# A graph network's node projection written out block by block, with gathers that wait for those of the last block, and half of the map-row gathers moved

## Time and profile before

| what | value |
|---|---|
| time, median of 3 runs | 4004.64 us (3991.43 to 4008.65) |
| the profiled execution | 4039.1 us, its span 4037.4 us |
| DVE busy | 2246.1 us, 56% of the span |
| POOL busy | 2168.0 us, 54% |
| PE busy | 2352.2 us, 58% |
| ACT busy | 1625.7 us, 40% |
| mean granted TensorE clock | 0.80 of 2.4 GHz |

### The profile page before, as it was taken

How to read it: one execution, slowest core, us unless ns; L and a number is a source line. 1 busy time by engine, 2 the same in 40 slices (tenths; PEclk the granted TensorE clock), 3 DMA queues, 4 the chain that set the end, 5 groups by cost and what they waited for, 6 DMA issues and landing times. The chain is left out here.

```text
span 4037.4 us, 57894 instructions
## 1 busy us (share of the span) xinstructions
PE 2352.2 (58%) x13633; PEld 1865.0 (46%) x13633; DVE 2246.1 (56%) x7631; ACT 1625.7 (40%) x3515; POOL 2168.0 (54%) x1921
## 2 busy tenths in 40 slices
PE   1136899899897664455646557775635433444333
PEld 1023676667677553354546445444624322333222
DVE  4145998899997665323422448885676323333223
ACT  0006999999995663222422323323421222222100
POOL 3628765566554770152055245555820488788755
PEclk9998999999999786587678668887866666666666
DMA  2140132233321543642455363333413433332243
GB/s 62 28 174 24 43 97 91 85 108 90 95 68 45 135 129 86 160 115 78 127 145 138 86 178 99 93 89 89 113 29 90 119 72 72 73 73 64 50 142 113
DMA packets 569016, 380.34 MB, mean 94 GB/s; under 512 B 51389, under 2 KB 511942, under 8 KB 568386
## 3 DMA queue, kind: packets, MB, share of 16 engines
q1 hardware_dynamic: 510050, 329.99, 27.7%
q0 software_dynamic: 56000, 46.29, 6.1%
q10 hardware_dynamic: 2720, 1.23, 0.2%
HBM read 249.08 MB, written 153.32 MB: 100 GB/s over the span
## 5 line engine op out<-in xcount | busy, mean ns | idle before, releaser
L1147 POOL DMA_INDIRECT p_ends_state<-t_d,p_ends_ix x300 | 315.6, 1052 | 543.9 <-issue 243.7
L806 POOL TENSOR_TENSOR a_rs<-a_ve,w_neg_half 128x16 f32<-128x16 f32 x113 | 330.4, 2924 | 244.8 <-DVE a_ve L742 214.9
L1367 PE MATMUL p_pm<-w_aug,p_ht 128*128 128x130 f32 (+1 forms) x1600 | 331.8, 329 | 173.0 <-ACT p_ht L1321 117.2
L832 ACT ACTIVATE a_nr<-a_xb,a_nm,a_rs 128x128 f32<-128x128 f32 x882 | 371.6, 490 | 26.1 <-POOL a_nm L808 26.1
L1367 PEld LDWEIGHTS p_pm<-w_aug,p_ht 128*128 128x128 f32 x1600 | 275.7, 234 | 194.9 <-issue 137.3
L1983 POOL DMA_INDIRECT e_a<-t_d,e_ix x200 | 211.7, 1059 | 269.7 <-DMA e_a<-t_s 206.9
L894 PE MATMUL a_ps<-w_ident,a_nr 128*128 128x128 f32 x1568 | 248.1, 282 | 127.8 <-ACT a_ht L840 46.9
L902 PE MATMUL a_ps<-a_ht,w_aug 128*128 128x512 f32 x588 | 315.6, 622 | 2.4 <-DVE a_ht L709 2.4
L894 PEld LDWEIGHTS a_ps<-w_ident,a_nr 128*128 128x128 f32 x1568 | 181.6, 144 | 276.7 <-issue 245.1
L709 DVE TENSOR_TENSOR a_ht<-a_ps,a_ht 128x512 f32<-128x512 f32 x294 | 203.1, 694 | 137.4 <-ACT a_ps L847 119.2
L1708 PE MATMUL c_pq<-layer_src,c_sel 128*128 (+1 forms) x800 | 194.3, 420 | 126.7 <-ACT c_sel L1679 83.5
(11 more groups left out here) (359 smaller groups left out, 6657.2 us busy)
## 6 DMA issues: line engine op xcount, KB each, us to landing
t_s<-p_ends_state SPq DMA_DIRECT2D x100, 256.0 KB
c_a<-t_d SPq DMA_DIRECT2D x100, 256.0 KB
t_d<-c_a SPq DMA_DIRECT2D x100, 256.0 KB
a_xa<-in_x SPq DMA_DIRECT2D x98, 256.0 KB
out<-a_xb SPq DMA_DIRECT2D x98, 256.0 KB, 2.0
p_ends_state<-t_s SPq DMA_DIRECT2D x75, 256.0 KB
p_ends_state<-t_d SPq DMA_DIRECT2D x75, 256.0 KB
t_acc<-q_zt SPq DMA_DIRECT2D x3, 2171.5 KB
```

The source lines that it names most:

```text
L806: nc.gpsimd.tensor_tensor(RS[:, z, :], VE[:, z, :], w["neg_half"][:, None, 0:J].to_broadcast([P, LNS, J]), ALU.pow).then_inc(s_rstd.sem, 1)
L832: last = nc.scalar.activation(NR[k][:, T.at(NORM[k], 2), cols(j)], normed_rows(T, k)[:, cols(j)], ACT.Identity, bias=NM[:, T.at(1, SHORT), ...
L1147: eng.indirect_dma_start(out=self.A[:, g, SRC, j, :], out_offset=None, in_=self.t[self.dst_table], in_offset=bass.IndirectOffsetOnAxis(ap= ...
L1367: last = nc.tensor.matmul(PM[side][:, j, 0:CW], HT[:, g, side, j * C:(j + 1) * C], rhs, start=side == SRC, stop=True)
```

## The change

- `project` is written out: all 25 blocks of each engine in straight code, no loop, no registers. The ring A has 7 blocks, the buffers behind it 3. SP issues all seven loads first; then, for each block b, store(b) and load(b + 6), and the xs rows of block b + 3.
- Overlay gathers read their index straight from `map_ix`; the copies L1139 are gone. Before the four gathers of block b POOL waits for the block's loads and, for each of the four columns j, for `s_over[j]` to reach 16 b: all four gathers of block b - 1 have landed.
- The inverse root moves from POOL to DVE: a new class `Moments` computes it with integer arithmetic on the float's bits as a first value and three Newton steps, in 12 steps (13 instructions) of 128 x 8 elements. Eight of the steps stand each behind one of the next block's eight statistics, four behind every second of its aggregates. A step waits for the one before it.
- ACT now normalises both sides (8 instructions a block, relu included for "first"); DVE writes both `layer_src` and `layer_dst` with the bias added (`hold`); the bias products on PE are gone. DVE's order is, for "first" and "normed": statistics with Newton steps, residual (lag 4), holds (lag 3); for "plain": residual (lag 1), holds (lag 0).
- The map-row gathers of `project` r = 0 are the first 50 alone, two per block, each pair behind the normalised destination side of a block. The other 50 stand on POOL in the `aggregate` phase of r = 0, two per block of that phase. They write straight into the int32 table `found`, so the casts are gone from `project`; `rows_found` runs after that aggregate phase and copies three more columns to float.

The diff, cut to its core:

```diff
@@ -477,11 +477,12 @@
                 ins_.then_inc(s_v, 1)
                 eng.wait_ge(s_v, n[0])
-            done(v.tensor_copy(k["map_ix"][:, :], f["found"][:, 0:T, 0]))
-            done(v.tensor_copy(OWNER[:, :], f["found"][:, 0:T, 1]))
+            done(v.tensor_copy(k["map_ix"][:, :], f["found"][:, :, 0]))
+            done(v.tensor_copy(OWNER[:, :], f["found"][:, :, 1]))
             for j in range(1, J):
-                done(v.tensor_tensor(OWNER[:, :], OWNER[:, :], f["found"][:, 0:T, 1 + j], ALU.min))
+                done(v.tensor_copy(TMP[:, :], f["found"][:, :, 1 + j]))
+                done(v.tensor_tensor(OWNER[:, :], OWNER[:, :], TMP[:, :], ALU.min))
             done(v.tensor_tensor(OWN[:, :], OWNER[:, :], f["number_f"][:, :], ALU.is_equal))
             done(v.tensor_scalar(TMP[:, :], k["src_col"][:, :], float(-SKIP), None, ALU.add))
...
+    def newton(self, eng, b, step):
+        v, g = self.nc.vector, b % self.ring
+        ve, half, square, y = self.var_eps[:, g, :], self.half[:, g, :], self.square[:, g, :], self.rstd[:, g, :]
+        if step == 0:
+            eng.wait_ge(self.s_moments, b + 1)
+            v.tensor_scalar(ve, self.moments[:, g, :, 1], LN_EPS, None, ALU.add).then_inc(self.s_newton, 1)
+            return
+        eng.wait_ge(self.s_newton, b * (self.STEPS - 1) + step)
+        if step == 1:
+            v.tensor_scalar(half, ve, -0.5, None, ALU.mult)
+            v.tensor_scalar(y.bitcast(I32), ve.bitcast(I32), -0.5, 1597463007.0, ALU.mult, ALU.add).then_inc(self.s_newton, 1)
+        elif step == self.STEPS - 1:
+            v.scalar_tensor_tensor(self.shift[:, g, :], self.moments[:, g, :, 0], -1.0, y, ALU.mult, ALU.mult).then_inc(self.s_shift, 1)
+        elif step % 3 == 2:
+            v.tensor_tensor(square, y, y, ALU.mult).then_inc(self.s_newton, 1)
+        elif step % 3 == 0:
+            v.tensor_tensor(square, square, half, ALU.mult).then_inc(self.s_newton, 1)
+        else:
+            v.scalar_tensor_tensor(y, square, 1.5, y, ALU.add, ALU.mult).then_inc(self.s_newton, 1)
+    def turn(self, eng, rows, b, last):
+        v = self.nc.vector
+        step = 0
+        for n in range(self.n):
+            if b <= last:
+                ins_ = v.bn_stats(self.stats[:, b % self.ring, n, :], rows(n))
+                if n == self.n - 1:
+                    ins_.then_inc(self.s_stats, 1)
+            if b and step < self.STEPS:
+                self.newton(eng, b - 1, step)
+                step += 1
+        if b <= last:
+            eng.wait_ge(self.s_stats, b + 1)
+        for n in range(self.n):
+            if b <= last:
+                ins_ = v.bn_aggr(self.moments[:, b % self.ring, n, :], self.stats[:, b % self.ring, n, :])
+                if n == self.n - 1:
+                    ins_.then_inc(self.s_moments, 1)
+            if n % 2 and b and step < self.STEPS:
+                self.newton(eng, b - 1, step)
+                step += 1
+        assert not b or step == self.STEPS
...
+            def load(b):
+                g = b % RING
+                if b >= RING:
+                    eng.wait_ge(s_out[g], (uses(b) - 1) * OUTS)
+                    eng.wait_ge(s_mm[DST], b - RING + 1)
+                for side in (SRC, DST):
+                    eng.dma_start(A[:, g, side, :, :], block_rows(t[tables[side]], b)).then_inc(s_load[g], 16)
+            def load_x(b):
+                if b >= SHORT:
+                    eng.wait_ge(s_plus, b - SHORT + 1)
+                eng.dma_start(XS[:, b % SHORT, :, :], block_rows(t["xs"], b)).then_inc(s_xs[b % SHORT], 16)
...
+            for b in range(RING):
+                load(b)
+                if plus_x and b < SHORT:
+                    load_x(b)
+            for b in range(BLOCKS):
+                store(b)
+                if b and b - 1 + RING < BLOCKS:
+                    load(b - 1 + RING)
+                if plus_x and b + SHORT < BLOCKS:
+                    load_x(b + SHORT)
+            for g in range(RING):
+                eng.wait_ge(s_out[g], OUTS * len(range(g, BLOCKS, RING)))
+        if overlay:
+            @block.gpsimd
+            def _(eng):
+                for b in range(BLOCKS):
+                    g = b % RING
+                    eng.wait_ge(s_load[g], uses(b) * 32)
+                    if b:
+                        for j in range(J):
+                            eng.wait_ge(s_over[j], 16 * b)
+                    for j in range(J):
+                        eng.indirect_dma_start(out=A[:, g, SRC, j, :], out_offset=None, in_=t[f"d{r}"],
+                                               in_offset=bass.IndirectOffsetOnAxis(ap=k["map_ix"][:, b * J + j:b * J + j + 1], axis=0),
+                                               bounds_check=EP - 1, oob_is_err=False).then_inc(s_over[j], 16)
+        if first:
+            @block.gpsimd
+            def _(eng):
+                for n in range(0, T // 2):
+                    eng.wait_ge(s_normed[DST], n // 2 + 1)
+                    eng.indirect_dma_start(out=f["found"][:, n, :], out_offset=None, in_=t["maps"].rearrange("(n a) o -> n (a o)", a=WORDS),
+                                           in_offset=bass.IndirectOffsetOnAxis(ap=f["map_at"][:, n:n + 1], axis=0),
+                                           bounds_check=NODES - 1, oob_is_err=False).then_inc(s_found, 16)
+                eng.wait_ge(s_found, 16 * (T // 2))
...
+            def hold(b):
+                for side in (SRC, DST):
+                    eng.wait_ge(s_mm[side], b + 1)
+                    v.tensor_tensor(held(("src", "dst")[side], b)[:, :, 0:CW], PM[side][:, :, 0:CW], wide, ALU.add).then_inc(s_keep[side], 1)
+            def residual(b):
+                g, grow = b % RING, UP[:, b % SHORT, :, :] if sigmoid else held("src", b)[:, :, 0:C]
+                if sigmoid:
+                    eng.wait_ge(s_sig, b + 1)
+                else:
+                    eng.wait_ge(s_keep[SRC], b + 1)
+                if plus_x:
+                    eng.wait_ge(s_xs[b % SHORT], (b // SHORT + 1) * 16)
+                    v.tensor_tensor(grow, grow, XS[:, b % SHORT, :, :], ALU.add).then_inc(s_plus, 1)
+                    eng.wait_ge(s_plus, b + 1)
+                there(eng, b, SRC)
+                v.tensor_tensor(A[:, g, SRC, :, :], A[:, g, SRC, :, :], grow, ALU.add).then_inc(s_next, 1)
+            holds, residuals = (3, 4) if norm else (0, 1)
+            for n in range(BLOCKS + residuals):
+                if norm and n <= BLOCKS:
+                    if n < BLOCKS:
+                        there(eng, n)
+                    mo.turn(eng, lambda m: A[:, n % RING, m // J, m % J, :], n, BLOCKS - 1)
+                if 0 <= n - residuals:
+                    residual(n - residuals)
+                if 0 <= n - holds < BLOCKS:
+                    hold(n - holds)
+            def apply(b):
+                g, m = b % RING, b % SHORT
+                eng.wait_ge(mo.s_shift, b + 1)
+                if normed and b >= SHORT:
+                    eng.wait_ge(s_mm[DST], b - SHORT + 1)
                 for side in (SRC, DST):
+                    for j in range(J):
+                        n = side * J + j
+                        rows = A[:, g, side, j, :]
+                        last = nc.scalar.activation(NR[:, m, side, j, :] if normed else rows, rows, ACT.Identity if normed else ACT.Relu,
+                                                    bias=mo.shift[:, m, n:n + 1], scale=mo.rstd[:, m, n:n + 1])
+                    last.then_inc(s_normed[side], 1)
...
@@ -1600,6 +1665,19 @@
+        if first:
+            s_found = sem("found")
+            @block.gpsimd
+            def _(eng):
+                for n in range(T // 2, T):
+                    if n >= T // 2 + 4:
+                        eng.wait_ge(s_next, (n - T // 2 - 2) // 2)
+                    eng.indirect_dma_start(out=f["found"][:, n, :], out_offset=None, in_=t["maps"].rearrange("(n a) o -> n (a o)", a=WORDS),
+                                           in_offset=bass.IndirectOffsetOnAxis(ap=f["map_at"][:, n:n + 1], axis=0),
+                                           bounds_check=NODES - 1, oob_is_err=False).then_inc(s_found, 16)
+                eng.wait_ge(s_found, 16 * (T // 2))
         if plus_x:
             @block.gpsimd
             def _(eng):
@@ -2256,10 +2334,10 @@
         keep, (wm, ws) = held(nc, ctx, "layer0", C + 2), softmax_weights(nc, ctx, "layer0", 1)
         for r in range(3):
             project(nc, w, k, t, r, 1, w["aug0"][:, r, :], w["b0_rows"][:, r, :], "plain" if r else "first", r == 2, keep, f)
+            attend(nc, w, k, r, 1, keep, wm, ws, True)
+            aggregate(nc, w, k, t, r, "sigmoid", 1, keep, wm, ws, r == 2, r == 0, f)
             if r == 0:
                 rows_found(nc, k, f)
-            attend(nc, w, k, r, 1, keep, wm, ws, True)
-            aggregate(nc, w, k, t, r, "sigmoid", 1, keep, wm, ws, r == 2, r == 0)
 def layers12_at_edges(nc, w, k, t):
```

(1 more changed line is left out.)

224 lines of the change are left out of this document (80 added, 144 removed).

## The result

The changed kernel takes 4062.05 us (median, 4058.36 to 4075.62) against 4005.76 us before: ratio 1.0154, 95% interval 1.012 to 1.0188. It is slower by 56 us; the forecast was 6 us faster, with a range up to 4042. Its profiled execution took 4058.36 us (span 4056.1).

What follows compares the result with a forecast made beforehand. POOL's gather chain was taken to pace the first and normed projections, stalls to lengthen the plain ones. Terms -41 + 3 + 13 + 14 + 4 + 1 = -6 us gave 3998 from 4004.64; own range 3980 to 4018, eight-in-ten range 3948 to 4042.

Steps and rivals of the forecast that it cites:

- L: Plain and normed phases: time from the fourth gather's busy end until landed; taken as 2.1 us, 2.2 with a third load.
- rival B: Plain and normed phases: landings meet the block's own store and loads, L = 2.7, +35 us, 4040; chance 0.18.
- the sign named beforehand: Forecast is wrong if a plain phase lies over 15 us from 214, or the first projection takes over 180.
- First plain phase: First plain projection: 24 periods of 7.9 us plus start and end, 214 us against 211, +3.
- Second: Second plain projection: 24 periods of 8.0 us plus start and end, 219 us against 206, +13.
- Normed: Normed projection: POOL period 8.0 us a block against 7.4, including 0.1 for a late load, +14 us.
- First projection: First projection: DVE becomes the bound, 5.7 us a block against 7.4, -41 us, bounds -55 and +22.
- Rival C: First projection misses 5.7 us a block, through small DVE instructions' waits or ACT's pace: +18 us, 4022; chance 0.08.
- The gathers in the aggregate phase and the bookkeeping: Half of the map-row gathers moved to the aggregate phase, +4 us; three more copies in row bookkeeping, +1 us.
- E: Plain and normed phases: the landing wait does not pace, phases keep their length; -36 us, 3969; chance 0.07.
- D: Plain phases: stalls of PE's products stay beside the landing wait, +58 us in each of two, 4115; chance 0.03.
- The stalls go (...), and the landing wait takes what they gave: First plain phase: ACT's waits for PE's products, 57.9 us, end as POOL's runs are cut to four gathers; net +3.

Runs made afterwards that it cites:

- Experiment 3: Changed kernel, landing wait kept, overlay phases' stores and loads shifted beside a later block's first gather, 9 ring buffers in the normed phase: ratio 1.0104 to before.
- experiment 6: Changed kernel with 9 ring buffers instead of 7 in the normed projection: ratio 1.0309 with the landing wait, 0.9709 without, to the kernel before.
- experiment 10: First kind of chip: changed kernel without landing wait, ratio 0.9907; kernel before with plain projections written out, the second without index copies, 0.994.
- the combination of 9: Changed kernel without landing wait, with 9 ring buffers in the normed projection and the first projection's inverse root by POOL's power: 3715.28 us, ratio 0.9674 to before.

## Why the prediction was wrong

*The step that failed* is the size of L, "I take the middle of 1.6 and 2.7, L = 2.1". Measured as in the earlier trace rows, from the end of the fourth gather to the start of its consumer, it was 2.9 in the first plain phase, 3.4 in the second and 2.9 in the normed one (means). A second, smaller size went the other way: the sum adds 0.9 of wake-up behind that start, but POOL starts only 0.51 us after PE's transposes (1747.14 and 1747.65), because PE's start holds a wake-up of its own. Counted to the landing itself, from the periods of after less 5.76 (4.9 and the wake-up 0.86), L was 2.6 in the first plain phase and 3.2 in the second.

That is rival B: it named the residual, the store and the loads that each landing releases, and gave 4040 for L = 2.7. Its mechanism is right; that its price comes near is in part luck, since L was higher and the wake-up lower, and 4062 still lies 22 us above it. Experiment 3 shows it: L = 1.45 with the same transfers at another moment. I wrote the phase relation down ("issued some 3 us after a landing") and then took it as "in flight for about half of the gathers' own time". The number that counts is not how long they are in flight but whether they are when the fourth gather is: issued some 3 to 6 us after the landing they were, in each block that had loads. The rows taken under loads, 2.6 to 2.7, were the nearer ones, and the phases came out above them. For the second plain phase, with the xs load as a third, the row with 4.8 stood in the earlier trace rows and was left out of the range. That phase also gave the sign named beforehand: 238 us is more than 15 away from 214.

*First plain phase,* +3 forecast, +14 measured: 24 x (8.40 - 7.9) = 12, where 11 us were missed: the period alone. *Second:* 24 x (8.93 - 8.0) = 22, where 20 were missed. *Normed:* 24 x (8.76 - 8.0) = 18 of the 24 missed; some 8 to 9 us belong to late loads, which I had at 0.1 x 24 = 2, the rest of the 18 to L. The other 6 us are a term that the sum put at nothing: from the end of the last gather to the end of the phase it takes 25.6 us (2974.3 to 2999.9), where before took 19.2. The waits name landing and loads:

```profile
POOL p_a L1309 <- DMA p_a<-t_d: 57.8, 11, 13.9
POOL p_a L1309 <- DMA p_a<-t_d,k_map_ix: 48.5, 14, 5.9
```

The first of the 11 waits for loads is the phase's start (13.9); ten more take (57.8 - 13.9) / 10 = 4.4 us each, where the 14 for a landing take 48.5 / 14 = 3.5. Nine buffers took 14 us off on the second kind of chip (experiment 6).

*First projection:* -47 against -41; from the first to the last of its 25 shifts (1316.4 to 1448.3) the period is 5.50 where 5.7 was forecast. The 13 small instructions cost 0.05 each, below the 0.10 taken and far from 0.30: the timeline of after has eight statistics, 13 small ones and eight aggregates from 1400.88 to 1404.00, 3.12 us for a forecast of 3.7; less the 1.64 and 0.78 of the earlier trace rows that leaves 0.70 for the 13.

```profile
1400.88 0.28 DVE L1203 BATCH_NORM_STATS2 p_mo_st<-p_a 128x6 f32<-128x128 f32 x1
1401.08 0.16 DVE L1181 TENSOR_SCALAR p_mo_ve<-p_mo_mv 128x8 f32<-128x8 f32 x1
1401.14 0.29 DVE L1203 BATCH_NORM_STATS2 p_mo_st<-p_a 128x6 f32<-128x128 f32 x1
...
1404.00 0.68 DVE L1356 TENSOR_TENSOR p_a<-p_a,p_up 128x512 f32<-128x512 f32 x1
```

Rival C fell with it. *The gathers in the aggregate phase and the bookkeeping* were right within 2 us and 0.3. E fell: the wait does pace. D fell on both kinds of chip, as long as there is a wait: with runs of four, after has no long wait on a product of PE but the one at each phase's start.

*A step that was right on one chip only:* "The stalls go (...), and the landing wait takes what they gave". On the first chip, stalls did end with the change, but the 211 and 205 us were no property of the kernel: the same code takes 151 and 173 on the other. I took the profile of one execution on one chip as the kernel, though the profile itself named no cause. With the phases of the second kind the sum would have been -41 + (214 - 151) + (219 - 173) + 16 + 5 = +89 us (16 is 208 + 14 - 206 for the normed phase), slower by more than 2% even at L = 2.1; measured there, 127.

*Landing and load.* L was 1.45 with store and loads beside the first gather and 2.6 to 3.2 with them beside the fourth. The Trainium skill (page "DMA: Bandwidth & Descriptors", section "Latency and other measured facts": HBM access 0.2 us on average, 2 us at high load) lets L grow with the load, and the traces agree. The fixed 2.0 us of its section "Anatomy of one DMA" gave L = 1.15, an estimate; the blocks of experiment 3, the shortest here, have 1.45.

*Open:* what makes hand-overs between engines late on the first kind of chip while POOL issues indirect transfers. The runs show when (unbroken runs, 28 gathers in experiment 10) and in which phases, not by which path; nor whether it is the chip itself or something else that differed between the groups. Whether the combination of 9 wins as much there was not tried; the landing wait is a loss there too in the plain phases (225 and 238 us with it, 188 and 197 without), and 7 us shorter with it in the normed one (245 against 252; one trace each).

## What to carry to other kernels

A wait for the landing of a transfer costs the issue, the landing and the wake-up in a row; before adding one, compute the period from the landing under the loop's own traffic, and note at which moment of the period that traffic starts: a self-releasing loop puts it at nearly the same place in every block. What matters is which gather the traffic stands beside, and whether anything waits for that one. In the plain phases one block of distance in the wait (the last but one) cost nothing and hid all of it. If a profile's longest waits name a releaser that makes no sense, look whether they are there on another chip before counting them as time that a change can win.

## What the runs showed of the hardware

The same program differs by 4% between chips (4006 and 4009 us in two groups, 3838 to 3842 in three), and the difference stands in phases in which POOL issues indirect transfers in long unbroken runs while PE and others hand over work: 251 against 179, 211 against 151, 205 against 173 us. The phase with four gathers between POOL's other work took 207 and 206, a phase of the edges 695 on both. A gather of 128 rows of 512 B landed in most blocks 1.3 to 1.5 us behind POOL's busy time with no load beside it or with a store alone, 2.3 to 3.5 beside two loads of 256 KB, and 4 to 5 at a phase's start beside ten or more loads. From the last increment of its semaphore POOL's next instruction took 0.86 us to start, PE's 0.35 and DVE's 0.22. TensorE's granted clock followed the waiting: 0.69 in the plain phases with the landing wait, where PE idled between blocks, 0.80 to 0.81 without it.
